# A two-phase decoder layer: cross-attention's sums by way of DRAM, its last projection a turn later, its value products one step later

## The reference

```python
x = _layernorm(x + _L0_attn_ref(x, w_project, w_out))            # 16 heads of 16, causal, 64 rows a sequence
x = _layernorm(x + _L0_xattn_ref(x, ctx, Wq, bq, Wk, bk, Wv, bv, Wo, bo))
x = _layernorm(x + _L0_ffn_ref(x, w1, b1, ln_g, ln_b, w2, b2))   # quantised 256 -> 1024 -> 256

def _L0_xattn_ref(x, c, ...):   # the 64 sequence rows are the channels: 8 heads of 8, over 256 positions
    q, k, v = split_heads(_proj(x, Wq, bq)), split_heads(_proj(c, Wk, bk)), split_heads(_proj(c, Wv, bv))
    q, k = _apply_rotary(q_emb, q), _apply_rotary(k_emb, k)
    p_attn = softmax(einsum('bhtc,bhsc->bhts', q, k) / sqrt(8))
    out = einsum('bhts,bhsc->bhtc', p_attn, v)
    return _proj(out, Wo, bo)
```

## Time and profile before

| | |
|---|---|
| three runs | 563.51, 562.63, 567.56 us; median 563.51 us |
| the profiled execution | 563.8 us, of which the span from first to last instruction is 561.9 us |
| phase A | 0 to about 417.8 us of the span |
| phase B, first stage | about 417.8 to 451 us |
| phase B, second stage | about 451 to 561.9 us |

### The profile page before, as it was taken

The page is one execution under the profiler, slowest core; times in us unless marked ns, Lnnn a source line. Parts: engine busy times, 40 slices in busy tenths (PEclk is TensorE's granted clock), DMA queues, the critical chain, the costliest instruction groups (busy, mean ns, idle before and its releaser), DMA issues. The chain is left out here.

```text
span 561.9 us, 12026 instructions
## 1 busy us (share of the span) xinstructions
PE 450.6 (80%) x4162; PEld 243.0 (43%) x4162; DVE 442.4 (79%) x965; ACT 382.0 (68%) x698; POOL 289.6 (52%) x387
## 2 busy tenths in 40 slices
PE   6568799999999999999999999889877701555563
PEld 5354545555545555555555555433333200333342
DVE  2656687888988979889889798865848959999973
ACT  2222266767767667676676686687767787999972
POOL 5742565447555574475555744620032727667652
PEclk9677799999999999999999999975987875555555
DMA  6134318233242242332422323210000000000010
GB/s 217 48 97 149 97 46 248 66 92 91 57 111 67 64 110 60 90 91 60 108 69 64 106 61 82 71 56 1 3 1 1 1 0 1 10 28 19 30 37 29
DMA packets 51674, 37.07 MB, mean 66 GB/s; under 512 B 21408, under 2 KB 47648, under 8 KB 51488
## 3 DMA queue, kind: packets, MB, share of 16 engines
q1 hardware_dynamic: 51328, 36.10, 22.8%
q10 hardware_dynamic: 288, 0.23, 0.2%
HBM read 24.52 MB, written 10.49 MB: 62 GB/s over the span
## 5 line engine op out<-in xcount | busy, mean ns | idle before, releaser
L970 DVE TENSOR_REDUCE MX<-mx_b 128x2 f32<-128x512 f32 x256 | 167.8, 679 | 37.6 <-PE mx_b L581 36.4
L775 ACT ACTIVATE PB<-e_b 128x512 f32<-128x512 f32 x256 | 149.6, 592 | 64.7 <-PE e_b L609 63.8
L581 PE MATMUL mx_b<-KA,QA 48*128 48x256 bf16 x512 | 100.8, 282 | 10.3 <-DVE MX L970 10.1
L609 PE MATMUL e_b<-QA,KA 50*128 50x256 bf16 x512 | 100.9, 281 | 2.7 <-ACT PB L775 2.1
L626 PE MATMUL u_b<-PB,VA 128*32 128x256 f32 x1024 | 86.2, 404 | 3.4 <-ACT PB L775 2.9
L897 POOL TENSOR_TENSOR SP<-SP,srec 128x1024 f32<-128x1024 f32 x15 | 28.5, 1901 | 79.0 <-DVE srec L942 79.0
L581 PEld LDWEIGHTS mx_b<-KA,QA 48*128 48x128 bf16 x512 | 30.1, 95 | 88.5 <-issue 48.9
L1238 POOL TENSOR_TENSOR H<-H,row_tab 128x1024 f32<-128x1024 f32 x16 | 37.8, 2359 | 22.9 <-ACT H L1196 19.5
L1285 PE MATMUL r_b<-identh,Q 128*128 128x128 f16 x128 | 16.6, 311 | 39.5 <-ACT Q L1206 39.5
L1291 PE MATMUL z_b<-w2q,Q2T 128*128 128x256 bf16 x128 | 30.2, 417 | 19.3 <-ACT Q2T L1217 19.3
L314 POOL TENSOR_TENSOR rs<-mv,epsc 128x1 f32<-128x1 f32 x32 | 6.1, 189 | 72.5 <-DVE mv L301 50.2
(11 more groups left out here) (169 smaller groups left out, 1048.4 us busy)
## 6 DMA issues: line engine op xcount, KB each, us to landing
KA<-parts_k SPq DMA_DIRECT2D x64, 96.0 KB
QA<-parts_q SPq DMA_DIRECT2D x64, 96.0 KB
parts_q<-part_q SPq DMA_DIRECT2D x32, 128.0 KB, 2.0
parts_k<-part_k SPq DMA_DIRECT2D x16, 192.0 KB, 2.1
C<-in_ctx SPq DMA_DIRECT2D x16, 128.0 KB, 3.0
X<-in_x SPq DMA_DIRECT2D x16, 128.0 KB, 2.9
out_y<-O SPq DMA_DIRECT2D x16, 128.0 KB, 1.7
XT<-in_xT SPq DMA_DIRECT2D x15, 128.0 KB, 2.2
```

The lines of the kernel that those rows point to most:

```text
L581: m = nc.tensor.matmul(mx_b[n % 2][:, D * k:D * k + D], QA[low:low + K_MAX, 2 * i.ring + b, h, P * u:P * u + P], KA[low:low + K_MAX, 2 * i ...
L609: m = nc.tensor.matmul(e_b[n % 2][:, D * k:D * k + D], KA[low:low + K_EXP, 2 * i.ring + b, h, P * sc:P * sc + P], QA[low:low + K_EXP, 2 * ...
L775: nc.scalar.activation(PB[:, n % 4].rearrange("p e t -> p (e t)"), e_b[n % 2][:, :], ACT.Exp, scale=XC ** -0.5).then_inc(e_sb.sem, 1)
L970: nc.vector.tensor_reduce(MX[:, b, e, 2 * q:2 * q + 2, u], mx_b[n % 2][:, :].rearrange("p (e s) -> p e s", e=2), AXL.X, ALU.max).then_inc( ...
```

## The change

- **Sums through DRAM.** `u_transpose`, `att_transpose`, `at_copy` and `u_norm` go. After each `u_copy`, SP stores `US` (256 KB) to a DRAM buffer (`store_sums`). `load_sums` reads it back as `S32` (the sums of exponentials, 128 x 32) and `UV` (the values, with channels and positions regrouped, 128 x 256). VectorE inverts `S32` (`reciprocals`); `recip_out` and `recip_in` send that through DRAM again to spread it over channels (`RB`); GpSimd multiplies (`means`). The weights of the last projection are permuted to fit, on the host. The values' bias goes through the last projection once, in turn 0 (`value_bias`).
- **The last projection a turn later.** `x_out_proj`, `norm2_stats`, `rstd`, `norm2`, `square_sum` and `norm2_max` now work on late = i-2. In turn 15 pair 13's are brought forward to steps 5 to 9, and pair 14's projection and statistics are put at step 15.
- **Value products one step later.** `pv_quad` m of turn i stands at step 2m+3 in place of 2m+2, quad 7 at step 1 of the next turn; `u_copy` follows. Around it `qk_proj` moves from step 1 to 0, `rotary_proj` of k from 9 to 8 and `v_proj` from 12 (before `transpose_p`) to 14.
- **C a turn ahead.** `load_c(i+4)` late in turn i in place of `load_c(i+3)` early in it; `expand_rows` of k moves from the end of a turn to the beginning of the next, behind `store_sums` and `max_rows`.
- **Feed-forward's first stage.** The last pair's chain is spread: `reciprocals` at t 5, projection at 8, `norm2_stats` at 9, `norm2` at 10, `norm2_max` at 12, `factors` of group 2 at 14 (before: 1, 3, 4, 5, 7, 9); pair 14's `norm2`, `norm2_max` and factors are now there too.
- `identb` is now made by two copies in place of one addition.

```diff
+        def store_sums(sp, i, b):
+            if has(i, 2):
+                sp.wait_ge(ld_uv, 16 * (i.v - 1))
+                sp.wait_ge(ld_us, 16 * (i.v - 1))
+            wait(sp, u_sb, i, b + 1)
+            sp.dma_start(u_hbm[i.p][:, :, b].rearrange("c j x -> j c x"), US[:].rearrange("p s t -> p (s t)")).then_inc(moved[b], 16)
+
+        def load_sums(sp, i):
+            if has(i, 1):
+                wait(sp, at_sb, i.plus(-1), 1)
+            for b in range(2):
+                sp.wait_ge(moved[b], 16 * (i.v + 1))
+            flat = u_hbm[i.p].rearrange("c j b x -> c (j b x)")
+            sp.dma_start(S32[:], flat[XC:XC + 1].rearrange("c (r t) -> (c r) t", t=32)).then_inc(ld_us, 16)
+            sp.dma_start(UV[:], flat[0:XC].rearrange("c (r t) -> (c r) t", t=D)).then_inc(ld_uv, 16)
+
+        def recip_out(sp, i):
+            wait(sp, u_rec, i, 1)
+            if has(i, 1):
+                sp.wait_ge(rec_in, 16 * i.v)
+            sp.dma_start(rec_hbm.rearrange("h (k t) -> (h k) t", t=32), S32[:]).then_inc(rec_out, 16)
+
+        def recip_in(sp, i):
+            sp.wait_ge(rec_out, 16 * (i.v + 1))
+            sp.dma_start(RB[:], rec_hbm.unsqueeze(0).broadcast_to([XC, 16, D])).then_inc(rec_in, 16)
+
+        def reciprocals(dve, i):
+            dve.wait_ge(ld_us, 16 * (i.v + 1))
+            nc.vector.reciprocal(S32[:], S32[:]).then_inc(u_rec.sem, 1)
+
+        def means(pool, i):
+            pool.wait_ge(ld_uv, 16 * (i.v + 1))
+            pool.wait_ge(rec_in, 16 * (i.v + 1))
+            if has(i, 1):
+                wait(pool, xo_ps, i.plus(-1), 1)
+            nc.gpsimd.tensor_tensor(AT[:], UV[:], RB[:], ALU.mult).then_inc(at_sb.sem, 1)
...
 (SP's body)
-                if i.v >= 1 and real(a):
-                    load_c(a)
+                if real(prev):
+                    store_sums(sp, prev, 1)
                 if real(i):
                     max_rows(i, 1)
+                if i.v == NPAIR - 1:
+                    load_sums(sp, prev)
+                    recip_out(sp, prev)
+                    recip_in(sp, prev)
+                if i.v >= 0 and real(j):
+                    expand_rows("k", j)
                 if real(a):
                     cross_values(a)
+                if real(prev) and real(nxt):
+                    load_sums(sp, prev)
                 if real(j):
                     store_parts("q", j)
+                if real(i):
+                    store_sums(sp, i, 0)
...
+                if real(prev) and real(nxt):
+                    recip_out(sp, prev)
                 if real(a):
                     store_parts("k", a)
...
+                if i.v >= 0 and real(i.plus(4)):
+                    load_c(i.plus(4))
+                if real(prev) and real(nxt):
+                    recip_in(sp, prev)
...
 (TensorE's body)
-                    if s == 0 and real(prev):
+                    if s == 0 and fresh(a):
+                        qk_proj(a, g_b[2])
+                    if s == 1 and real(prev):
                         pv_quad(prev, 7)
-                    if s == 1 and fresh(a):
-                        qk_proj(a, g_b[2])
...
-                    if s == 3 and real(prev):
-                        u_transpose(pe, prev, 1, use(g_b[2], u_nrm, prev, 4))
...
-                    if s == 5 and real(prev):
-                        att_transpose(pe, prev, use(g_b[2], at_sb, prev, 1))
...
-                    if s == 9 and fresh(a):
+                    if s == 8 and fresh(a):
                         rotary_proj("k", g_b[2], a)
-                    if s == 9 and real(prev):
-                        x_out_proj(pe, prev, use(g_b[1], ln2, prev, 1))
+                    if s == (9 if real(nxt) else 5) and real(late):
+                        x_out_proj(pe, late, use(g_b[1], ln2, late, 1))
...
-                    if s == 12 and real(i.plus(4)):
-                        v_proj(i.plus(4), g_b[0])
                     if s == 12 and real(a):
                         transpose_p(a)
-                    if s == 13 and real(i):
-                        u_transpose(pe, i, 0, use(g_b[1], u_nrm, i, 2))
...
+                    if s == 14 and real(i.plus(4)):
+                        v_proj(i.plus(4), g_b[0])
                     if s == 15 and real(a):
                         out_proj(a)
-                    if s and s % 2 == 0 and real(i):
+                    if s >= 3 and s % 2 and real(i):
                         pv_quad(i, s // 2 - 1)
+                    if s == 15 and i.v == NPAIR - 1:
+                        x_out_proj(pe, prev, use(g_b[2], ln2, prev, 1))
...
 (VectorE's body)
-                    if s == 3 and real(prev):
-                        u_norm(dve, prev, 1, 2)
+                    if s == 11 and real(prev):
+                        reciprocals(dve, prev)
...
-                    if s == 10 and real(prev):
-                        norm2_stats(dve, prev, 1)
-                    if s == 13 and real(i):
-                        u_norm(dve, i, 0, 1)
+                    if s == (10 if real(nxt) else 6) and real(late):
+                        norm2_stats(dve, late, 1)
+                    if s == 13 and i.v == NPAIR - 1:
+                        factors(dve, 0)
+                    if s == 15 and i.v == NPAIR - 1:
+                        norm2_stats(dve, prev, 2)
...
 (GpSimd's body, between split_parts of q and self_norm)
+                if real(late) and real(nxt):
+                    means(pool, late)
...
 (feed-forward, TensorE)
             pe.wait_ge(s_tab, 4)
-            u_transpose(pe, last, 1, g_b[1])
             for t in range(TURNS1):
-                if t == 2:
-                    att_transpose(pe, last, g_b[0])
-                if t == 3:
+                if t == 8:
                     x_out_proj(pe, last, g_b[1])
```

More of the change, by code:

```diff
@@ L842, in body @@
                         exp_tile(i, s)
-                    if s == 0 and real(prev):
-                        u_copy(prev, 1)
                     if s == 0 and real(j):
@@ L857, in body @@
                         self_exp(a, 0)
-                    if s == 8 and real(i):
+                    if s == 9 and real(i):
                         u_copy(i, 0)
@@ L863, in body @@
                         pt_copy(a)
-                    if s == 13 and real(prev):
-                        norm2(act, prev)
+                    if s == (13 if real(nxt) else 8) and real(late):
+                        norm2(act, late)
+                    if s == (15 if real(nxt) else 8) and real(late):
+                        square_sum(act, late)
                     if s == 13 and real(a):
@@ L1385, in _ @@
             nc.vector.memset(base[:], 1.0).then_inc(s_base, 1)
-            mean_square(dve, 1)
             for t in range(TURNS1):
-                if t == 1:
-                    u_norm(dve, last, 1, 1)
-                if t == 4:
+                if t == 3:
+                    norm2_max(dve, last.plus(-1))
+                    mean_square(dve, 1)
+                if t == 5:
+                    reciprocals(dve, last)
+                if t == 7:
+                    factors(dve, 1)
+                if t == 9:
                     norm2_stats(dve, last, 1)
-                    factors(dve, 1)
-                if t == 7:
+                if t == 12:
                     norm2_max(dve, last)
@@ L1406, in _ @@
         def _(sp):
+            load_sums(sp, last)
+            recip_out(sp, last)
+            recip_in(sp, last)
             for n in range(NPAIR):
```

132 lines of the change are left out of this document (63 added, 69 removed).

## The result

The changed kernel takes 594.9 us (median; its runs 592.4 to 596.8) against 564.7 us before: a ratio of 1.052 (95% interval 1.046 to 1.059), slower by 5%. Forecast were 574.5 us and 562 to 590: the sign is right, the time is 20 us above the forecast and 5 us above the range. The profiled execution took 595.07 us with a span of 592.9. Ratios leave out disturbed executions, so one need not be the quotient of two medians; that matters for e12 alone.

The account below looks back on a forecast made before the run. TensorE and VectorE were taken to bound different stretches of a turn. 563.8 + 14.1 (turns 0 to 12) - 4 (13 and 14) + 2.5 (15) - 2 (feed-forward) = 574.4, stated as 574.5 us; range 562 to 590.

Parts of the forecast that it names:

- The stretches: Turns 0 to 12, cut at heads of steps 4, 7, 9, 13: 23.65 us a turn, 1.16 more; +14.1 in all.
- 7 to 9: Between heads of steps 7 and 9, TensorE's work: rotary_proj of k comes in, 1.86 + 0.97 = 2.83 us.
- 13 to 4: Head of step 13 to next turn's step 4, TensorE's work: 10.20 us becomes 10.56.
- 9 to 13: Between heads of steps 9 and 13: both projections leave TensorE, but VectorE's chain holds it at 6.02 us, from 6.19.
- The rival of the clock: Main turns: TensorE's idle gaps make the clock fall, 1.5 us or more each, 13 x 1.5 = +20, about 590; chance 0.10.
- The six have room: SP's queue, 21 to 27 DMAs a turn: the six extra fit, stores landing 2.0 us after issue; priced at nothing.
- Turns 13 to 15: Last turns: removed transposes give -4 us in turns 13 and 14 together; turn 15's new DRAM chain costs +2.5.
- the term for turn 15's end: Turn 15: reciprocals, DRAM hops, GpSimd's product and projection come ahead of the last pv_quad: +2.5 us, bounds 0 and +5.
- First stage: Feed-forward's first stage: u_transpose and a VectorE wait go, pair 14's norm2_max and DMA chain come: -2 us, bounds -3.5 and +1.5.
- The second stage: Feed-forward's second stage: untouched, to about 1 us.
- the terms' bounds: Whole kernel: the terms' bounds together put the time at about 566 to 584 us.
- The first rival: TensorE bounds throughout, so removed work counts in full: 1.55 us in each of 13 turns, about 540 us; chance 0.12.

Follow-up runs that it names:

- e12: Changed kernel with k's rotary_proj back at step 9, v_proj back at step 12, and stores cut to 72 KB: 568.1 us, 0.997 of the kernel before.
- e7: Kernel before the change with only rotary_proj of k moved, from step 9 to 8: 579.0 us, 1.026.
- e8: Kernel before the change with only v_proj moved, from step 12 to 14: 583.5 us, 1.034.
- e4: Changed kernel with eight redundant matmuls added in each of steps 6 and 12 of turns 0 to 12: 586.9 us, 1.039 of the kernel before.
- e1: Changed kernel with rotary_proj of k back at step 9 and v_proj back at step 12: 585.5 us, 1.034 of the kernel before.
- e3: Kernel before the change, transposes kept on chip, with only the change's new placements of projections, pv_quad and u_copy: 594.7 us, 1.054.
- e11: Changed kernel, all places kept, with each store of the sums cut from 256 to 72 KB as four DMAs: 583.8 us, 1.034 of the kernel before.
- e13: Changed kernel with stores cut to 72 KB and redundant matmuls filling steps 6 and 12: 579.1 us, 1.025 of the kernel before.
- e9: Changed kernel with TensorE's and ScalarE's old places and stores cut to 72 KB as four DMAs: 552.9 us, 0.980 of the kernel before.
- e2: Changed kernel with TensorE's and ScalarE's places as before the change; DRAM route and later projection stay: 560.7 us, 0.994 of the kernel before.
- e10: Kernel of e2 with the whole 256 KB stores issued from ScalarE's queue, not SyncE's: 577.3 us, 1.021 of the kernel before.
- e14: Changed kernel with stores cut to 72 KB and redundant matmuls in step 6 alone: 582.3 us, 1.029 of the kernel before.
- e15: Changed kernel with stores cut to 72 KB and redundant matmuls in step 12 alone: 581.3 us, 1.027 of the kernel before.

## Why the prediction was right and wrong

**The stretches: right.** Removed TensorE work gave nothing where another engine sets the head, and moved work cost in full where TensorE does. In an undisturbed turn all four stretches were within 0.11 us. The 7 to 9 stretch was 0.09 short and 13 to 4 was 0.11 short, since a projection that I priced at 0.97 takes 1.06 where it now stands (e7, e8). So the clean turn came to 23.86 for 23.65: 2.5 us over twelve turns. In 9 to 13 there was some luck: I had VectorE's chain as the only limit, and in e7 and e8 ScalarE and GpSimd set the head 0.15 us behind it; in the changed kernel too TensorE first waits 1.04 us for GpSimd.

**The rival of the clock: under-weighted.** This is one of the two steps that failed: the sum has the granted clock staying at its full level, with no term for the gaps that the change opens. The rival was named with its mechanism, place and price (1.5 us or more a fall), and given 0.10. Measured: six falls in the twelve turns, about 10 us of the 12 that they were over the forecast; filling the gaps gave 8 (e4). I argued against it that the gaps are apart. That is no defence: each fall follows a single gap, and in e1 and e12 one gap of 1.39 us a turn was enough for it, in some turns and not in others. The transposes that go had filled part of the gap before head 7 (1.02 us with them in e3, 1.39 without), and e3 had no fall in its main turns; that this 0.37 us makes the difference is likely, not shown, as e3 also lacks the traffic with DRAM. The error was in giving the sum no share of a rival that pulls only one way. The rival's 590 us is wrong as a sum, too: 574.5 and its 13 x 1.5 make 594, outside the stated range. That this meets the measured 595 is luck, since only six falls came in the twelve turns, and the last turns brought the rest.

**"The six have room": wrong.** This is the other failed step. I priced the DMA hops at nothing, by their number in SyncE's queue and by the landing time of 128 KB. A store here is 256 KB, lands 6.5 us after issue, and the 4 KB rows right behind it don't land before. I had looked at what is queued behind the waiting instruction, but not at what lands behind a slow transfer. The rows behind it make TensorE wait 1.7 and 2.7 us in the last turns, and the store makes ScalarE wait 3.5. A warning lay in the diff: per turn 2 x 256 KB written, where 128 KB and a row of sums are read. The cut store gave 11 us to the changed kernel (e11); 5.6 of them can be placed, in turns 12 to 15 (75.5 to 69.9).

**Turns 13 to 15.** Forecast -1.3 with turn 12, measured +7.3. Between successive copies of `u_b` (turn 12's `ssum`, first half of 13, of 14, of 15, last copy, feed-forward):

| | before | after | e11 | e13 |
|---|---|---|---|---|
| to first half of 13 | 20.9 | 23.4 | 21.1 | 19.8 |
| to first half of 14 | 23.6 | 23.7 | 22.2 | 22.2 |
| to first half of 15 | 15.6 | 17.9 | 16.1 | 15.0 |
| to the last copy | 7.0 | 8.5 | 7.8 | 7.4 |
| to feed-forward | 1.0 | 2.1 | 2.6 | 2.6 |

In e13 this part is 67.0 us, a 1.2 us gain as forecast; -4 for turns 13 and 14 was about right (-3.1 with turn 12's end, all three rows together), and the term for turn 15's end, +2.5, too (+0.4 and +1.6: SyncE still issues the last store before the barrier). What the changed kernel has on top of that is late row maxima, late stores and a lower clock.

**Feed-forward.** First stage -2.8 us against -2. The second stage was 1.6 us shorter; it has a stretch at full clock (581.8 to 588.6 us) near its end, where the clock stayed low before. I had left it alone.

**Together.** The forecast's sum describes the profiled execution of e13 to a microsecond in every line of the first table but the main turns (+1.9). That execution is the shortest of its four, and e13's median of 579.1 is 4.6 us above the forecast. So it was a fair sum for a kernel without two things, the gaps' effect on the clock and the landing of the stores, and what is left is no more than e13's own scatter. Two slips in it are small: the 0.3 us by which the profiled execution lies above the median should have been taken off (574.1), and the terms' bounds add up to 565 to 586, not 566 to 584.

The first rival (all of the removed work counts) did not come true even with nothing moved: in e9 and in e2's undisturbed turns 1.16 us a turn came in, the two `u_transpose` of the stretch 13 to 4, and not the 1.55 of all removed instructions.

## What to carry to other kernels

Before moving work in a pipeline of near-level engines, cut the turn at the instructions that wait for another engine: work taken out of such a stretch is worth next to nothing (0.03 us for 0.97 here), work put into the others costs in full. If TensorE gets gaps, ask what a fall of the clock behind them would cost (1.5 us each here), and give it a share of the sum. And a detour through DRAM is priced by the landing time of its own transfers and by what stands behind them, not by the row of another transfer; store only the rows that are read back.

## What the hardware showed that I had not expected

- A 256 KB store of 128 partitions landed 6.5 us after issue in a stretch where the queue did little else, while the 128 KB stores of parts took 2.2 us (2.0 before) and a load of 1024 KB 5.9. The DMA share was 0.24 meanwhile. 4 KB transfers issued 0.7 us behind it on the same queue took 5.8 us to be usable. With the store issued from another engine's queue such rows still took 5.1 to 7.8 us (e10), with the store cut 2.2 to 2.7 (e9).
- Behind single idle stretches of TensorE of 0.9 to 1.4 us the clock fell in some turns and not in others: six times in twelve turns of the changed kernel, with two such stretches a turn; seven and four times in e1 and e12, with the 1.39 us alone; once in 24 turns of e14 and e15, also with one. The twelve turns of e3, with 1.02 and 1.04 + 0.34 us idle, kept the clock.
- Adding 16 matmuls a turn whose results nobody reads made the kernel 8 us faster (e4).
